# A graph network on one core: one fixed item per tile of nodes, edges counted by comparing keys, own rows added by VectorE

## The chip, the cores and the metric

The kernel runs on one core of one Trainium2 chip. The metric is the device time of one execution in microseconds, the median of several runs. The engines are TensorE (PE, its weight loads PEld), VectorE (DVE), ScalarE (ACT), GpSimd (POOL) and SyncE (SP), whose queue issues most transfers.

## The reference, cut

Four layers on 50,000 nodes with 256 features and 25,000 edges (src, dst, two edge types, a weight), each followed by a layer norm of input plus output. What the change touches is the second and the third.

```
def rgcn_layer(x, src, dst, edge_type, W, root, bias):      # twice
    xj = x[src]; out = x @ root + bias
    for r in range(16):
        mask = (edge_type == r)
        s = segment_sum(xj * mask[:, None], dst)
        cnt = segment_sum(mask, dst)
        h = s / maximum(cnt, 1.0)[:, None]
        out = out + blockdiagonal(h, W[r])
...
rel_e = relation_emb[edge_type]
def agg(x):                                                  # two hops
    e = sum((concat(x[head], x[tail]) @ fc_w.T + fc_b) * rel_e)
    e = where(e > 0, e, 0.2 * e)
    ex = exp(e - segment_max(e, head)[head])
    w = ex / segment_sum(ex, head)[head]
    return segment_sum(x[tail] * w[:, None], head) + x
for _ in range(2):
    x = agg(x); x = x / maximum(norm(x), 1e-12)
```

## The kernel before

**Items.** The nodes lie in 391 tiles of 128. `sort_edges` sorts the edges by src (`by_src`) and by dst (`by_dst`) into items: an item is up to 128 edges that all have their node in one tile. A tile with more than 128 edges would have several items, one behind the other, and an empty tile has one. With the given edges no tile has more than 128 of them, so there are 391 items for 391 tiles. `Tables.make` works out on VectorE, for each of 640 possible items and both graphs, its tile (LOAD), where its result is stored (STORE), the last item of its tile (LAST) and whether it goes on with the sum of the item before (`keep`); `Tables.number` adds SLOT, the tile's place in its octet of eight. Everything behind reads these tables into registers, since where a tile's items lie depends on the edges.

**Stages.** They run one after the other, each in a block of its own: the sort with weights, `mean_layer` (l0), `count_edges_and_message` (ma), `relation_layer` (l1a), `message_phase` (mb), `relation_layer` (l1b), `attention_hop` twice (l2a, l2b), `interaction_layer` (l3).

**ma.** 216 chunks of 128 edges in pairs: GpSimd gathers rows of x (L1098) into 24 landing slots, TensorE turns them (L1220) and multiplies by the blocks of the edge type (L1229), ScalarE copies between the two, VectorE copies the products out (L1120), and SyncE stores them. mb does the same for the second layer (L1329 to L1397) with filler matmuls `keep_busy` (L772) between. In ma the edges of each node and type are counted beside this. For the first 48 pairs a group of 8 items is made into one-hot matrices (L1111, L1106), multiplied (L1244) and copied to `total` (L1191); 8 pairs carry 16 scans over `total` (L1160), which add up the items of a tile; in 48 more pairs each edge looks its count up: a transposed one-hot (L1125) by the totals (L1253), masked by type (L1130) and reduced (L1133). At the end the share is 1 over the count (L1179).

**Hops.** `attention_hop` works on octets (8 items), two octets being one hop of the loop; 48 octets are written out, two more run in a loop with registers, and `steps` is the written order of each engine, with how many octets each step runs ahead. Per octet: `find_nodes` compares the row of node names (L2057, L2059); `look_up` gets each edge's head projection (L2320); `scores` adds the gathered one (L2070 to L2077); `spread` lays masked scores out by node (L2298, L2300); `maximum` takes the peak (L2126) and carries a running maximum over the items of a tile (L2130 to L2143); `chances` is exp with an accumulated sum (L2212); `turn_chances` turns it back (L2307); `aggregate` multiplies by the gathered rows (L2288). The node's own row is added in `add_self` (L2100) on VectorE in the first hop and in `own_rows` on TensorE in the second, by a diagonal that GpSimd makes (L2025); `guarded` (L2083) is its weight. `add_up` (L2121, in the second hop L2118) adds the sum of the item before, shrunk by the change of the maximum (0 where a new tile begins). `measure` (L2199) and `InverseRoot` (L2147, L1721 to L1738) give the norm. The second hop adds the residual (L2155) and a layer norm. GpSimd gathers eight items per octet (L1989), each half of them when TensorE has aggregated the octet that lay there two octets before.

## Time and profile before

| | us |
|---|---|
| median of 3 timed runs | 6657.72 (6646.8 to 6664.31) |
| profiled execution, span | 6924.1 |
| PE / PEld / DVE / ACT / POOL busy | 6036.3 / 5008.9 / 5018.1 / 4517.3 / 3702.0 |

The profiled execution has one time, its span, which is 4% above the median of the timed runs. Busy shares of the span (87% for PE) are averages over nine stages with different limits, and are read stage by stage.

### The profile page before, as it was taken

The numbers are of one execution on the slowest core, as the hardware profiler recorded it, in microseconds if no ns is written. First come the engines' busy times: TensorE is split into PE (matmuls) and PEld (weight loads), VectorE is DVE, ScalarE is ACT, GpSimd is POOL, SyncE is SP. The second block draws the span as 40 slices with busy tenths as digits, with TensorE's granted clock in tenths as the row PEclk, the third lists the DMA queues.
The fourth block names the chain that finished last, engine by engine and source line by source line (L and its number), as shares of the span: only waits on it lengthen the run. The fifth ranks groups of instructions, "written<-read, shape, count | busy, mean of one in ns | idle before, by whom it ended". The sixth has DMA issues, their size and how long they took to land. (4 is left out here: it accounts for less than half of the span.)

```text
span 6924.1 us, 154954 instructions
## 1 busy us (share of the span) xinstructions
PE 6036.3 (87%) x34664; PEld 5008.9 (72%) x34665; DVE 5018.1 (72%) x17037; ACT 4517.3 (65%) x15396; POOL 3702.0 (53%) x3473
## 2 busy tenths in 40 slices
PE   6437999977899987899999788887888887999999
PEld 2226999966877775699999666665776766888888
DVE  9786999976555551277777677775666666898898
ACT  1866999952144441178888566665777776777777
POOL 0766777756366666544444444444554455444444
PEclk9658999988899998999999899998989998999999
DMA  1025777765566665577777566665666665444444
GB/s 39 2 6 162 211 210 211 211 187 163 164 184 189 192 182 166 163 215 220 218 221 219 167 203 201 198 200 158 206 198 194 196 203 175 117 127 125 126 126 119
DMA packets 1158773, 1173.00 MB, mean 169 GB/s; under 512 B 301535, under 2 KB 1032838, under 8 KB 1157701
## 3 DMA queue, kind: packets, MB, share of 16 engines
q1 hardware_dynamic: 1007108, 953.00, 45.3%
q0 software_dynamic: 151360, 216.47, 12.4%
q8 instruction: 127, 2.08, 0.1%
q14 instruction: 178, 1.45, 0.1%
HBM read 961.43 MB, written 392.14 MB: 195 GB/s over the span
## 5 line engine op out<-in xcount | busy, mean ns | idle before, releaser
L214 POOL DMA_INDIRECT landing_first<-messages,by_dst_meta x768 | 842.7, 1097 | 721.8 <-PE l1b_ps_b L1541 366.5
L214 POOL DMA_INDIRECT landing_last<-x,by_dst_meta x384 | 434.4, 1131 | 561.0 <-PE l_ps_a L1678 487.9
L1989 POOL DMA_INDIRECT landing_last<-z,by_src_meta x408 | 424.3, 1040 | 521.3 <-PE l2b_ps_g L2288 366.6
L1989 POOL DMA_INDIRECT landing_last<-x,by_src_meta x408 | 422.7, 1036 | 462.4 <-PE l2a_ps_g L2288 255.9
L214 POOL DMA_INDIRECT landing_first<-in_x,by_src_meta x384 | 407.7, 1062 | 196.7 <-PE l_ps_a L993 74.4
L1495 ACT ACTIVATE l1a_x_t<-l1a_ps_x,by_dst_first 128x256 f32<-128x256 f32 x400 | 168.0, 471 | 418.0 <-PE l1a_ps_x L1527 280.0
L1539 PE MATMUL l1b_ps_b<-root,l1b_x_t 128*128 128x256 f32 x1600 | 426.9, 389 | 1.4
L1539 PE MATMUL l1a_ps_b<-root,l1a_x_t 128*128 128x256 f32 x1584 | 418.1, 386 | 9.7 <-issue 6.1
L1003 PE MATMUL l_ps_b<-l_w,l_both 128*128 128x256 f32 x1624 | 419.3, 381 | 0.0
L1006 PE MATMUL l_ps_b<-l_w,l_agg_t 128*128 128x256 f32 x1624 | 418.0, 380 | 0.0
L1697 PE MATMUL l_ps_b<-l_w,l_mix_t 128*128 128x256 f32 x1592 | 396.6, 392 | 10.2 <-issue 7.7
L1447 DVE SCALAR_TENSOR_TENSOR l1a_total<-l1a_total,by_dst_keep,l1a_ps_b 128x256 f32<-128x256 f32 x394 | 187.1, 475 | 292.1 <-PE l1a_ps_b L1541 234.5
L1693 PE MATMUL l_ps_b<-l_w,l_x_t 128*128 128x256 f32 x1592 | 382.2, 383 | 2.5 <-ACT l_x_t L1658 2.5
L1697 PEld LDWEIGHTS l_ps_b<-l_w,l_mix_t 128*128 128x128 f32 x1592 | 286.2, 189 | 115.7 <-DVE l_mix_t L1614 63.1
L288 POOL DMA_INDIRECT item_records<-sort_rec,places x196 | 218.5, 1115 | 243.8 <-DVE places L596 184.5
L1006 PEld LDWEIGHTS l_ps_b<-l_w,l_agg_t 128*128 128x128 f32 x1624 | 309.6, 191 | 42.5
L1098 POOL DMA_INDIRECT landing_first<-x,rel_index x216 | 238.7, 1105 | 164.4 <-PE ma_ps_x L1220 83.9
L1539 PEld LDWEIGHTS l1a_ps_b<-root,l1a_x_t 128*128 128x128 f32 x1584 | 286.3, 191 | 55.0 <-issue 18.9
L772 PE MATMUL l2a_ps_g<-zero_row,ones_b 128*128 128x392 bf16 x1734 | 321.2, 329 | 1.1 <-issue 1.1
L1003 PEld LDWEIGHTS l_ps_b<-l_w,l_both 128*128 128x128 f32 x1624 | 294.1, 191 | 32.1
L1539 PEld LDWEIGHTS l1b_ps_b<-root,l1b_x_t 128*128 128x128 f32 x1600 | 289.6, 191 | 36.5 <-issue 3.7
L1693 PEld LDWEIGHTS l_ps_b<-l_w,l_x_t 128*128 128x128 f32 x1592 | 286.6, 190 | 33.8 <-ACT l_x_t L1658 2.9
(399 smaller groups left out, 19392.5 us busy)
## 6 DMA issues: line engine op xcount, KB each, us to landing
l_both<-in_x_both SPq DMA_DIRECT2D x416, 256.0 KB
l2a_x<-x SPq DMA_DIRECT2D x53, 1216.0 KB
z<-l2a_result SPq DMA_DIRECT2D x400, 152.0 KB
x<-l1b_result SPq DMA_DIRECT2D x392, 152.0 KB
l2b_x<-z SPq DMA_DIRECT2D x53, 1024.0 KB
l1b_x<-h SPq DMA_DIRECT2D x408, 128.0 KB
l1b_res<-x SPq DMA_DIRECT2D x408, 128.0 KB
l2b_res<-x SPq DMA_DIRECT2D x51, 1024.0 KB
```

The costliest lines, as they stand in the source:

```text
L214: pool.indirect_dma_start(gathered[:, slot, 0:D], None, source[0:count, :], bass.IndirectOffsetOnAxis(ap=rows, axis=0), bounds_check=limit ...
L288: self.pool.indirect_dma_start(self.target, bass.IndirectOffsetOnAxis(ap=self.place[:, column:column + 1], axis=0), self.source(column), N ...
L772: pe.matmul(spare, c.ones_b[:], c.zero_row[:], start=True, stop=True)
L1003: pe.matmul(ps_b[k % 4], x_t[:, m, i * P:(i + 1) * P], w[:, 2 + i, :], start=(i == 0), stop=False)
L1006: last = pe.matmul(ps_b[k % 4], agg_t[:, k, i * P:(i + 1) * P], w[:, i, :], start=False, stop=(i == 1))
L1098: pool.indirect_dma_start(gathered[:, slot, :], None, x_in[0:N_NODES, :], bass.IndirectOffsetOnAxis(ap=relations.index[:, chunk:chunk + 1] ...
L1447: dve.scalar_tensor_tensor(total[:, k, :], total[:, (k - 1) % RING, :], graph.keep[:, bass.ds(j, 1)], ps_b[k // 2 % 2][:, k % 2, :], ALU.m ...
L1495: act.activation(x_t[:, k, :], ps_x[k // 2 % 2][:, k % 2, :], ACT.Copy, scale=graph.first[:, bass.ds(j, 1)]).then_inc(s["xt"], 1)
L1539: pe.matmul(sums, x_t[:, k, f * P:(f + 1) * P], root[:, f, :], start=(f == 0), stop=False)
L1693: pe.matmul(ps_b[k % 4], x_t[:, k, i * P:(i + 1) * P], w1[:, i, :], start=(i == 0), stop=False)
L1697: last = pe.matmul(ps_b[k % 4], mix_t[:, k, i * P:(i + 1) * P], w2[:, i, :], start=False, stop=(i == 1))
L1989: pool.indirect_dma_start(gathered[:, k, :], None, x_in[0:N_NODES, :], bass.IndirectOffsetOnAxis(ap=rows, axis=0), bounds_check=limit, oob ...
```

## The change

Every tile now has exactly one fixed item, whose number is the tile's. Only tiles with more than 128 edges get items behind them (from 392 on), so the first 48 octets know their tile when the code is written: loads of x, heads and residual use constants, and no running sum or maximum is carried there. The possible items rise from 640 to 896, and SLOT and `Tables.number` go. In ma 384 items are counted by comparing keys (node times 16 plus type) of an item's 128 edges with each edge's own, 4 compares behind each copy; the remaining group keeps the old way, in a loop ahead of the pairs, and fillers stand where look-ups stood. In the second hop the own rows move to VectorE, as in the first. Some buffers now share memory with others that are idle at that time (in l0 and the sort).

```diff
-MAX_ITEMS = TILES + N_EDGES // P
+MAIN = TILES + 1
+MAX_ITEMS = MAIN + 2 * (N_EDGES // (P + 1))
...
+OCTETS_FIXED = HOPS_FIXED * 2
...
# Tables.make
+            for q in range(whole, ITEM_CHUNKS):
+                chain.step(dve.tensor_scalar(self.junk[:, 0:n], b["end"][:, 0:n], c.item_id[:, q:q + 1], 0.0, ALU.is_le, ALU.add,
+                                             accum_out=self.tile_id[:, o, q:q + 1]))
...
             for q in range(ITEM_CHUNKS):
-                chain.step(dve.tensor_scalar(self.junk[:, 0:n], b["end"][:, 0:n], item, 0.0, ALU.is_le, ALU.add,
-                                             accum_out=self.tile_id[:, o, q:q + 1]))
                 for what, out in (("base", self.base), ("end", self.end)):
...
# count_edges_and_message, VectorE
+                def compare(g, odd):
+                    if not odd:
+                        dve.wait_ge(key_in[g % 2], (g // 2 + 1) * 16)
+                    for k in range(odd * HALF, (odd + 1) * HALF):
+                        j = g * RING + k
+                        if j >= 2:
+                            dve.wait_ge(s["compared"], j - 1)
+                        dve.tensor_scalar(same[:, j % 2, :], key_row[:, g % 2, k, :], key[:, j:j + 1], 0.0, ALU.is_equal, ALU.add,
+                                          accum_out=graph.share[:, j:j + 1]).then_inc(s["compared"], 1)
...
-                for pair in range(SCANNED, LOOKED):
-                    take_message(pair)
-                    g = pair - SCANNED
-                    look_and_take(g, g % 2, g // 2)
...
+                for pair in range(SCANS_AT, PAIRS_ALL):
+                    take_message(pair)
+                    g, odd = divmod(pair - FIRST_LOOK, 2)
+                    if 0 <= g < FAST_GROUPS:
+                        compare(g, odd)
# the same, TensorE
-                    if pair < COUNTED:
-                        count(pair)
-                    elif SCANNED <= pair < LOOKED:
-                        look_up(pair - SCANNED, (pair - SCANNED) % 2)
+                    if SCANS_AT <= pair < PAIRS_ALL - 8:
+                        keep_busy(pe, c, ps_spare, 3)
                     if pair + 2 < PAIRS_ALL:
                         turn(pair + 2)
+                    if SCANS_AT <= pair < PAIRS_ALL - 8:
+                        keep_busy(pe, c, ps_spare, 3)
...
# attention_hop, SyncE
+                def load_tiles(octet, target, source, columns, loads):
+                    if octet.general:
+                        rows = rows_of("load", LOAD, octet)
+                        for q in range(OCT):
+                            sp.dma_start(target[:, q, :], source[bass.ds(rows[q], P), columns]).then_inc(loads[1][octet.half], 16)
+                    else:
+                        tiles = source[bass.ds(octet.item * P, OCT * P), :].rearrange("(k p) d -> p k d", p=P)
+                        sp.dma_start(target, tiles[:, :, columns]).then_inc(loads[0][octet.half], 16)
...
# GpSimd
-                    pool.tensor_tensor(diag[:, 0:own_pe, :], c.ident[:].unsqueeze(1).broadcast_to([P, own_pe, P]),
-                                       guarded[:, octet.half, 0:own_pe].unsqueeze(2).broadcast_to([P, own_pe, P]), ALU.mult)\
-                        .then_inc(s["diag"], 1)
...
# VectorE
-                        dve.scalar_tensor_tensor(like_sums(q, z[:, k, :]),
-                                                 like_sums(q, x[:, bass.ds(at[q] + o.base, 1), :].rearrange("p k d -> p (k d)")),
+                        dve.scalar_tensor_tensor(like_sums(q, z[:, k, :]), like_sums(q, x[:, k, :]),
                                                  guarded[:, o.half, q:q + 1], sums(q), ALU.mult, ALU.add).then_inc(s["mixed"], 1)

                 def add_up(o, h):
+                    if not o.general:
+                        return
...
                 def maximum(o):
...
+                    if not o.general:
+                        o.wait(dve, s["peak"])
+                        dve.tensor_scalar(below[:, o.half, :], peak[:, o.both], -1.0, -FLOOR, ALU.mult, ALU.min)\
+                            .then_inc(s["below"], 1)
+                        return
...
# TensorE, second hop
-                    steps = [(find_slots, 3), (find_own, 1), (part(own_rows, 0), 1), (part(aggregate, 0), 1), (part(own_rows, 1), 1)]
...
+                    steps = [(part(aggregate, 0), 1), (part(aggregate, 1), 1), (part(aggregate, 2), 1), (spread, 2), (part(aggregate, 3), 1),
+                             (part(fill, 16), 2), (part(turn_chances, 0), 2), (look_up, 3), (part(fill, 4), 2),
+                             (part(turn_chances, 1), 2), (part(fill, 4), 2)]
```

VectorE in ma, in the part where edges look their counts up. Before, one pair and its group of 8 items:

```order
L1120 COPY ma_message<-ma_ps_m 128x512
L1125 TENSOR_SCALAR ma_hot_t<-ma_row,item_id 128x1024
L1106 TENSOR_TENSOR ma_kind<-by_dst_meta,iota 128x128
L1130 TENSOR_TENSOR ma_own<-ma_kind,ma_ps_e 128x128
L1133 TENSOR_REDUCE by_dst_share<-ma_own 128x8
L1120 COPY ma_message<-ma_ps_m 128x512
```

Now, two pairs, with the compares of one group of 8 items between them:

```order
L1153 COPY ma_message<-ma_ps_m 128x512 x2
L1163 TENSOR_SCALAR ma_same,by_dst_share<-ma_key_row,ma_key 128x128 x4
L1153 COPY ma_message<-ma_ps_m 128x512
L1163 TENSOR_SCALAR ma_same,by_dst_share<-ma_key_row,ma_key 128x128 x4
L1153 COPY ma_message<-ma_ps_m 128x512
```

Per pair 4 compares of 128 elements stand where a 1024-element compare, a type mask, a product and a reduction stood for 8 items; a group's compares now span two pairs.

VectorE in the first hop, from the third sum of an octet to the end of its maximum. Before:

```order
L2100 SCALAR_TENSOR_TENSOR l2a_z<-l2a_x,l2a_guarded,l2a_ps_g 128x304
L2121 SCALAR_TENSOR_TENSOR l2a_z<-l2a_z,l2a_shrink 128x304 x3
L2126 TENSOR_REDUCE l2a_peak<-l2a_ps_e 128x8
L2130 SCALAR_TENSOR_TENSOR l2a_top<-l2a_restart,l2a_top,l2a_peak 128x8
L2133 TENSOR_TENSOR l2a_old_top<-l2a_top,l2a_restart 128x8
L2135 TENSOR_SCALAR l2a_below<-l2a_top 128x8
L2137 TENSOR_SCALAR l2a_empty<-l2a_top 128x8
L2140 TENSOR_TENSOR l2a_minus<-l2a_old_top,l2a_top 128x8
L2143 COPY l2a_top<-l2a_top 128x1
```

Now, from the weight of the own row (`guarded`) on:

```order
L2101 SCALAR_TENSOR_TENSOR l2a_guarded<-l2a_peak,l2a_share 128x8
L2114 SCALAR_TENSOR_TENSOR l2a_z<-l2a_x,l2a_guarded,l2a_ps_g 128x304 x3
L2132 TENSOR_REDUCE l2a_peak<-l2a_ps_e 128x8
L2135 TENSOR_SCALAR l2a_below<-l2a_peak 128x8
L2114 SCALAR_TENSOR_TENSOR l2a_z<-l2a_x,l2a_guarded,l2a_ps_g 128x304 x4
L2114 SCALAR_TENSOR_TENSOR l2a_z<-l2a_x,l2a_guarded,l2a_ps_s 128x304
```

The running sums L2121 are gone, and only the peak and its negation are left of the maximum.

TensorE in the second hop, at the start of an octet. Before (TENSOR_LOAD and ISA rows are its sequencer reading slots and waiting):

```order
L1831 TENSOR_LOAD by_src_table x2
L1834 ISA
L2275 ISA
L2275 MATMUL l2b_ps_g<-l2b_x,l2b_diag 128x256
L2275 ISA
L2275 MATMUL l2b_ps_g<-l2b_x,l2b_diag 128x256
L2288 MATMUL l2b_ps_g<-landing_last,l2b_hot 128x256 x2
L1834 ISA
L2275 ISA
L2275 MATMUL l2b_ps_g<-l2b_x,l2b_diag 128x256
```

Now, the whole pass up to the first turn of chances:

```order
L2277 MATMUL l2b_ps_g<-landing_last,l2b_hot 128x256 x6
L2287 MATMUL l2b_ps_e<-l2b_mask,ident_b 128x512
L2289 MATMUL l2b_ps_e<-ident,l2b_score 128x128 x4
L2287 MATMUL l2b_ps_e<-l2b_mask,ident_b 128x512
L2289 MATMUL l2b_ps_e<-ident,l2b_score 128x128 x4
L2277 MATMUL l2b_ps_g<-landing_last,l2b_hot 128x256 x2
L788 MATMUL l2b_ps_spare<-zero_row,ones_b 128x392 x16
L2296 MATMUL l2b_ps_e<-ident,l2b_chance 128x128 x4
```

The products with `l2b_diag` and the register reads are gone; six aggregations stand in a row, then the spread, the last two and 16 fillers.

## Rows read from the trace of the kernel before

**Rows 1.** Windows by stage: length, busy us by engine, PEclk, DMA share, GB/s.

```profile
1467.00:1893.00 426.00, 324.19 (x2498) 300.57 (x2498) 253.10 (x531) 83.11 (x216) 238.68 (x216) 0.81 0.58 169
...
2600.00:2935.00 335.00, 264.97 (x1872) 209.68 (x1872) 73.69 (x108) 60.15 (x108) 214.28 (x212) 0.95 0.54 162
...
3828.00:4770.00 942.00, 803.37 (x5060) 609.93 (x5060) 688.08 (x1779) 604.18 (x2315) 444.74 (x430) 0.96 0.63 191
...
4770.00:5871.00 1101.00, 956.76 (x5186) 757.40 (x5186) 734.91 (x2420) 815.43 (x3207) 552.55 (x532) 0.90 0.64 194
```

**Rows 2.** Groups by line, counting stage: busy us, mean ns, idle before.

```profile
L1120 DVE COPY ma_message<-ma_ps_m 128x512 f32<-128x512 f32 x108 | 74.1, 686 | 84.2 <-PE ma_ps_m L1229 53.7 <-remote 20.5 <-issue 9.5
...
L1179 DVE RECIPROCAL by_dst_share<-by_dst_share 128x640 f32<-128x640 f32 x1 | 4.2, 4152 | 0.0
```

**Rows 3.** Timeline, ends of both message stages: start us, duration us.

```profile
1468.70 1.01 POOL L1098 DMA_INDIRECT landing_first<-x,rel_index  x1 [23.25 <-POOLq L123]
...
1896.63 0.27 DVE L1477 MEMSET l1a_total<- 128x256 f32 x1 [0.85 <-PEq L123]
...
2594.95 1.01 POOL L1329 DMA_INDIRECT landing_first<-h,rel_index  x1 [9.29 <-POOLq L123]
...
2931.25 0.69 DVE L1397 COPY mb_message<-mb_ps_m 128x512 f32<-128x512 f32 x1 [0.44 <-PE mb_ps_m L1350]
```

**Rows 4.** Groups by line, first hop, 3900 to 4700 (46 octets).

```profile
L2121 DVE SCALAR_TENSOR_TENSOR l2a_z<-l2a_z,l2a_shrink 128x304 f32<-128x304 f32 x365 | 195.8, 536 | 23.3
...
L2070 DVE TENSOR_TENSOR l2a_both<-l2a_ps_s,landing_last 128x192 f32<-128x192 f32 x46 | 16.4, 358 | 35.1 <-DMA landing_last<-x,by_src_meta 28.9 <-issue 5.8
...
L2147 DVE TENSOR_SCALAR l2a_inv_v<-l2a_total_sq 128x8 f32<-128x8 f32 x46 | 7.9, 172 | 40.9 <-ACT l2a_squares L2199 40.9
```

**Rows 5.** Timeline, two passes of the first hop, VectorE and GpSimd.

```profile
4215.83 0.36 DVE L2070 TENSOR_TENSOR l2a_both<-l2a_ps_s,landing_last 128x192 f32<-128x192 f32 x1 [0.35 <-DMA landing_last<-x,by_src_meta]
...
4222.74 1.01 POOL L1989 DMA_INDIRECT landing_last<-x,by_src_meta  x1 [1.41 <-PE l2a_ps_s L2288]
...
4226.69 1.28 POOL L1989 DMA_INDIRECT landing_last<-x,by_src_meta  x1 [0.31 <-issue]
...
4233.06 0.36 DVE L2070 TENSOR_TENSOR l2a_both<-l2a_ps_s,landing_last 128x192 f32<-128x192 f32 x1 [1.18 <-DMA landing_last<-x,by_src_meta]
```

**Rows 6.** Groups by line, second hop, 4850 to 5800 (46 octets).

```profile
L2275 PE MATMUL l2b_ps_g<-l2b_x,l2b_diag 128*128 x724 | 194.8, 405 | 19.2 <-POOL l2b_diag L2025 17.4 <-issue 1.6
...
L2025 POOL TENSOR_TENSOR l2b_diag<-ident,l2b_guarded 128x1024 f32<-128x1024 f32 x46 | 87.7, 1906 | 3.6
...
L2147 DVE TENSOR_SCALAR l2b_inv_v<-l2b_total_sq 128x8 f32<-128x8 f32 x46 | 47.7, 1037 | 88.4 <-ACT l2b_squares L2199 38.9 <-DMA x<-l1b_result 38.2 <-issue 11.3
```

**Rows 7.** Timeline, second hop, one VectorE step and the diagonal beside it.

```profile
5211.70 1.85 DVE L2147 TENSOR_SCALAR l2b_inv_v<-l2b_total_sq 128x8 f32<-128x8 f32 x1 [1.27 <-issue]
...
5211.63 1.90 POOL L2025 TENSOR_TENSOR l2b_diag<-ident,l2b_guarded 128x1024 f32<-128x1024 f32 x1
```

**Rows 8.** Table of two neighbouring octets of the second hop.

```profile
5181.60:5200.30 18.70, 16.99 (x102) 13.25 (x101) 12.37 (x45) 12.02 (x47) 10.66 (x11) 1.00 0.61 187
...
5200.30:5224.50 24.20, 21.03 (x101) 16.96 (x101) 16.56 (x51) 18.27 (x74) 10.35 (x11) 0.79 0.61 183
```

**Rows 9.** Timeline, TensorE in these two octets.

```profile
5189.28 1.86 PE L2320 MATMUL l2b_ps_s<-l2b_head,l2b_hot_t 128*128 x16
...
5208.75 0.66 PE L2307 MATMUL l2b_ps_e<-ident,l2b_chance 128*128 128x128 f32 x4 [2.56 <-ACT l2b_chance L2212]
...
5210.82 3.45 PE L2320 MATMUL l2b_ps_s<-l2b_head,l2b_hot_t 128*128 x16
```

**Rows 10.** Tables of the sort: one wide step (by line), one small (timeline).

```profile
L376 DVE TENSOR_SCALAR_CACHE_REDUCE sort_in_relation<-dst_end,item_id 128x391 f32<-128x391 f32 x5 | 3.1, 620 | 3.5 <-remote 2.2 <-DVE by_src_groups L396 1.3
...
371.33 0.17 DVE L386 TENSOR_SCALAR sort_vals<-sort_end 128x5 f32<-128x5 f32 x1 [1.23 <-DVE sort_vals L385]
```

**Rows 11.** Timeline, SyncE's queue in the first hop: eight issues of one store.

```profile
4703.77 4.88 SPq L1939 DMA_DIRECT2D z<-l2a_result  x8
```

More of the change, by code:

```diff
@@ L413, in turn @@
         sp.wait_ge(s_rows, 160)
[L415 to L423 removed]
+        sp.wait_ge(s_table, 32)
 def by_item(records):
@@ L1082, in _ @@
                             .then_inc(row_in[h], 16)
-                for h in range(2):
-                    sp.wait_ge(row_in[h], ((groups + 1) // 2 + 1) * 16)
-                    sp.sem_inc(s["passed"], 1)
+                for pair in range(SCANS_AT, PAIRS_ALL):
+                    store(pair)
+                    g, odd = divmod(pair - FIRST_LOOK, 2)
+                    if odd and 0 <= g < FAST_GROUPS - 2:
+                        load_keys(g + 2)
+                with sp.Fori(FAST_GROUPS // 2, (groups + 1) // 2) as both:
+                    for h in range(2):
+                        sp.wait_ge(row_in[h], (both + (2 - FAST_GROUPS // 2)) * 16)
+                        sp.sem_inc(s["passed"], 1)
                 for n in range(R // 2):
@@ L1742, with __init__ @@
 class Octet:
-    def __init__(self, group, n):
+    def __init__(self, group, n, general=None):
         self.number = group * 2 + n
@@ L1752, in __init__, with landed @@
         self.dynamic = not isinstance(self.number, int)
+        self.general = general if self.dynamic else self.number >= OCTETS_FIXED
+        assert self.general is not None
+    def landed(self, loads):
+        if self.general:
+            return loads[1][self.half], (self.lap + (1 - HOPS_FIXED)) * (16 * OCT)
+        return loads[0][self.half], (self.lap + 1) * 16
     def each(self):
@@ L1826, in attention_hop @@
         restart = ph.sb("restart", [P, ITEMS], F32)
-        diag = ph.sb("diag", [P, OCT, P], F32) if own_pe else None
         res = ph.sb("res", [P, OCT, D], F32) if last_hop else None
-        def load_slots(eng, regs, octet):
-            eng.load(regs, graph.table[0:1, SLOT, bass.ds(octet.item, OCT)])
-        def slots_of(eng, regs):
-            return [eng.snap(r, min_val=0, max_val=OCT - 1) for r in regs]
         ps_e = ph.ps("e", [P, OCT, P])
@@ L1924, in load_heads @@
                         sp.sem_inc(s["passed"], 1)
-                    sp.dma_start(head[:, octet.both, :], tiles[:, :, D + R2:]).then_inc(in_head[octet.half], 16)
+                    load_tiles(octet, head[:, octet.both, :], x_in, slice(D + R2, ROW), in_head)
                 def load_res(octet):
-                    tiles = tiles_of("res", octet, residual)
                     if octet.after(1):
@@ L1931, in load_res @@
                         sp.sem_inc(s["passed"], 1)
-                    sp.dma_start(res[:], tiles[:, :, 0:D]).then_inc(in_res[octet.half], 16)
+                    load_tiles(octet, res[:], residual, slice(0, D), in_res)
                 def store(octet):
@@ L2202, in decay @@
                 def decay(o):
+                    if not o.general:
+                        return
                     o.wait(act, s["minus"])
```

443 lines of the change are left out of this document (198 added, 245 removed).

## The prediction

> **What bounds the kernel now.** I read the table of stages first [rows 1]. The stages run one after the other, and the change touches the sort, the counting stage and both hops. In each row the reader is to see the busy time of every engine beside the length of the stage, then the granted TensorE clock. ScalarE, VectorE and GpSimd are full in none; TensorE is the fullest engine in both hops (803 of 942 us, 957 of 1101 us), but in the counting stage it is only 76% busy, at clock 0.81. So I went on stage by stage, to the groups by line and then to the order in time.
>
> The counting stage (1467 to 1893) and the second message stage (2600 to 2935) do the same 108 pairs of products from the same 216 gathers; only the first also counts edges. From the first gather to the end of the last copy the pure stage takes 2594.95 to 2931.94, 337.0 us or 3.12 a pair. The counting stage takes from 1468.70 to 1896.63, where the next stage's first instruction starts, 427.9 us [rows 3]. The difference is what counting costs.
>
> In the first hop one octet follows the other at 17.23 us (the same VectorE step at 4215.83 and 4233.06 [rows 5]); the window gives 942 us / 53 passes = 17.8 (50 octets and 3 lead-in passes). Two loops have this length. One is VectorE's own order, in which the running-sum step L2121 takes 8 x 536 ns = 4.3 us per octet [rows 4]. The other goes through GpSimd: gathers released at 4222.74, the fourth issued at 4226.69, VectorE waiting 1.18 us for its landing until 4233.06 [rows 5], then score, spread, aggregation and the next release. VectorE waits for landings 28.9 us in 46 octets [rows 4], so neither loop alone sets the pass.
>
> In the second hop a pass takes 1101 / 53 = 20.8 us. Per octet TensorE is busy 957 / 50 = 19.1 us, ScalarE 815 / 50 = 16.3, VectorE 14.7 [rows 1]. Two neighbouring octets show the two forms of a pass: 18.7 us at clock 1.00 and 24.2 us at 0.79 [rows 8]. In the long one the turn of the chances comes 2.56 us late, and then the same 16 look-up matmuls take 3.45 us in place of 1.86 [rows 9]. TensorE is the bound, and waiting for ScalarE makes it slower still. GpSimd's diagonal, 1906 ns, lies over a VectorE instruction on 8 elements that takes 1.85 us, where the first hop's takes 0.17 [rows 4, 6, 7].
>
> **The change part by part.** *Sorting and tables.* The wide VectorE steps at 128x391, about 0.62 us each [rows 10], go from 5 x 3 to 4 + 7 x 2 per graph, 30 to 36 in all: +4. The chain of small steps grows by about 28 in the tables and 8 in the buckets. One costs 0.17 us of work, and 1.4 with the wait for its neighbour's result [rows 10]: 36 x 0.17 = 6 to 36 x 1.4 = 50 us. About a third of these steps wait fully, so I take 14, and 2 for record loads that are 1.4 times as long: **+20** (10 to 50). GpSimd waits for the places that come out of the buckets and hides nothing of their part; of the tables it hides what is done before its last scatter. The removed numbering of octets runs beside those scatters and gives nothing back.
>
> *Counting stage.* 48 of 49 groups lose one-hot count, scan and look-up, and get 8 compares of 128x128 each with an accumulated sum, 4 behind each copy of the later pairs. No row shows this form. The nearest is L376, the same operation at 391 elements, 0.62 us, which bounds it from above; 0.17, the price of a handful of elements, does from below [rows 10]. By element count between them: 0.17 + 0.45 x 128 / 391 = 0.32 us. VectorE then does 0.69 [rows 2] + 4 x 0.32 = 2.0 us a pair, under the 3.12 at which the pure stage goes; the gathers and TensorE cover it. At 0.66 with spacing a pair takes 3.3 and costs 0.2 x 96 = 19 us. Ahead of the pairs stand four more transposes and one counted group; the gathers run on meanwhile into 24 landing slots, so of that delay I take 3 (0 to 14). Behind them the share of 896 items in place of 640: 4.15 x 1.4 = 5.8 [rows 2], with small steps 7.5, and the last compares 1. End: 1468.7 + 337.0 + 3 + 7.5 + 1 = 1817.2 against 1896.6: **-79** (-90 to -45).
>
> *First hop.* L2121 goes for 48 octets, and with it running maximum, its old value, the reset and ScalarE's decay: about 5 us of VectorE per octet. Only what the gather loop leaves of that is worth something. There the landing takes 4233.06 - 4226.69 = 6.4 us from the fourth gather's issue. The 1216 KB load of x stands in the same engines and will be issued earlier, since it waits for the sums of the octet before. With the landing as now a pass is 17.2 (gain 0.6, all of it from slower passes than the one shown); with landings no longer late, TensorE's busy time bounds at 803 / 50 = 16.1 (gain 1.7). I take 17.0, nearer to the loop that the rows show: 0.8 x 50 = 40. At the hop's end the general form loads tile by tile. Eight issues of a store take 4.88 us on that queue [rows 11], and eight each for x and heads now stand between them, in two octets: +10. **-30** (-80 to +10).
>
> *Second hop.* Own rows leave TensorE: 194.8 / 46 = 4.2 us per octet [rows 6]. In the octet at full clock it was busy 17.0 of 18.7 us [rows 8], so 12.8 remain. VectorE takes the own row into the instruction that added the running sum before, so its count there stays. GpSimd loses the diagonal, and L2147 goes from 1037 back to 172 ns [rows 4, 6]. What is late next is ScalarE: 16.3 us of work per octet, less 0.2 for the decay, plus waits in its ring: about 17.0. TensorE will then stand still 4 us per octet, in pieces that can be as long as the 2.56 us behind which its clock fell [rows 9]. One such fall cost 24.2 - 18.7 - 2.6 = 2.9 us of stream [rows 8, 9]; the slack hides a part, and I add 1.3. So 18.3 in place of 20.8: 2.5 x 50 = 125. The end costs more than in the first hop, since the residual is loaded by tiles too: +15. **-110** (-205, at ScalarE's 16.3, to -45).
>
> *Sum.* +20 - 79 - 30 - 110 = -199 on the profiled span of 6924.1 us. The timed runs have a median of 6657.7, 0.962 of it, so -191: **6465 us**.
>
> **The rivals.** *The first hop stays on its gather loop* (chance 0.15), since the load of x, issued earlier, collides with the gathers. For it: VectorE already waits for landings. Against it: 28.9 us in 46 octets are little beside 5 us per octet. No gain there: 6465 + 40 x 0.962 = 6505 us.
>
> *The second hop stays at 20.8* (0.17): a loop through landing, score and spread, or TensorE's uneven clock, takes the place of the own rows. For it: this hop moves 194 GB/s over 20.8 us, and its engines' share of 0.64 would be 0.76 at 17.5 [rows 1]. Against it: passes of 18.7 exist with the own rows in them. 6465 + 120 = 6585 us.
>
> *The compares are dear* (0.07). At 0.85 us each, the 0.62 and a wait for the compare two before, a pair takes 4.1 us, and the 79 us are gone: 6541 us.
>
> *TensorE's clock stays down in the second hop* (0.03); this one ends on the other side. The counting stage shows clock 0.81 at 76% busy, the second message stage 0.95 at 79% [rows 1]; the new hop would be busy 13 of 17 us, 76%. If the engine stays at the lower of its two levels (1.2 GHz), 12.8 us double to about 26, a pass is 26 in place of 20.8, +260 us, and the sum is -199 + 125 + 260 = +186 on the span: 6837 us. It decides from a pass of 22.3 on, where the other gains are used up. The Trainium skill says in "TensorE: Matmul & The Clock Gate", part 1, that the lower level is the default and activity releases the upper one; by that rule less work on this engine is a danger in itself. This case's octets agree in that the clock falls behind an idle stretch [rows 8, 9]; the octet ahead of that stretch is at the full one, fillers and all.
>
> **How the numbers follow.** My forecast, each term within its bounds, has 0.56; the rivals 0.15, 0.17, 0.07 and 0.03; 0.02 is for what I have not thought of. The best bounds together would be 10 - 90 - 80 - 205 = -365, or 6307 us; the first three rivals reach 6505 to 6585. With no more than two in ten outside I keep 6355 to 6580. About 0.3% (20 us) is what a measurement of this kernel can tell from no change; all cases but the last are faster by more. Faster 0.95, same 0.02, slower 0.03.
>
> **What would show it.** The counting stage at 349 us, its copies 3.1 us apart, the 128-element compare near 0.32 us. The first hop at 17.0 a pass, with VectorE idle 4 us more per octet and waiting for landings. The second hop at 18.3 a pass, L2147 at 0.17 us, TensorE idle 4 us with its clock under 0.95. The tables 15 us longer. I am wrong if the compare takes over 0.6 us, if a pass of the second hop stays above 20, or if the hops' ends cost more than 40 us together.

## The result and the profile after

The changed kernel takes 6409.31 us (median of 4 runs, 6404.78 to 6418.08) against 6653.1 of the kernel before: ratio 0.9632, 95% interval 0.9619 to 0.9646, 244 us faster. The forecast was 6465. The page of its profiled execution begins so (span, then busy us by engine, with shares of the span):

```profile
span 6403.0 us, 147348 instructions
PE 5706.8 (89%) x33252; PEld 4755.8 (74%) x33253; DVE 4656.3 (73%) x16722; ACT 4458.0 (70%) x15208; POOL 3534.5 (55%) x3365
```

One thing has to be known for all that follows: the profile from which the forecast was made (span 6924.1) was of a disturbed execution, and a second profile of the same kernel has a span of 6639.6 us. So the stages are compared with that second profile. Its windows of the counting stage, the first hop and the second hop (each from the end of the stage ahead, or its own start, to the start of the next; length, busy us of PE, PEld, DVE, ACT, POOL, then PEclk, DMA share, GB/s), where [rows 1] had 426, 942 and 1101:

```profile
1415.70:1817.50 401.80, 316.37 (x2498) 297.31 (x2498) 253.65 (x531) 84.29 (x217) 243.53 (x216) 0.84 0.61 181
3669.80:4588.10 918.30, 772.76 (x5008) 601.30 (x5060) 685.93 (x1780) 609.16 (x2316) 440.56 (x430) 0.98 0.65 196
4588.10:5590.90 1002.80, 902.98 (x5134) 717.33 (x5186) 734.30 (x2421) 817.74 (x3207) 556.52 (x532) 0.94 0.70 213
```

The same three windows of the changed kernel:

```profile
1415.90:1723.90 308.00, 261.43 (x1902) 221.31 (x1902) 212.21 (x917) 67.57 (x125) 220.56 (x216) 0.92 0.80 238
3571.70:4444.60 872.90, 786.95 (x5060) 607.22 (x5060) 454.19 (x1179) 587.10 (x2268) 431.50 (x430) 0.97 0.68 206
4444.60:5355.50 910.90, 748.88 (x4370) 600.89 (x4370) 637.63 (x2280) 806.36 (x3159) 442.00 (x428) 0.89 0.78 234
```

The reader is to see 401.8 become 308.0, 918.3 become 872.9, and 1002.8 become 910.9. All other stages together, from the sort to the last layer, give 5.5 us. The sum is 6639.6 - 6403.0 = 237 us on the spans.

The sort shows why its term is missing. The second profile of before, the last VectorE step of the sort and GpSimd's last scatter:

```profile
456.53 0.48 DVE L422 TENSOR_SCALAR by_dst_table<-sort_rows_on 1x640 int32<-1x640 int32 x1
...
501.01 0.97 POOL L288 DMA_INDIRECT item_records<-sort_rec,places  x1 [0.30 <-issue]
```

And the changed kernel:

```profile
465.01 0.36 DVE L652 TENSOR_SCALAR rel_index<-sort_ps_source 128x216 int32<-128x216 f32 x1
...
500.11 0.96 POOL L289 DMA_INDIRECT item_records<-sort_rec,places  x1 [0.30 <-issue]
```

VectorE's last step starts 8 us later and has 35 us to spare before the scatters end; the next step waits for those, and they end within 1 us of where they did.

The counting stage in order of time (GpSimd's gathers, VectorE's copy of a pair, its first compares, the next gather and copy):

```profile
1600.21 1.00 POOL L1131 DMA_INDIRECT landing_first<-x,rel_index  x1 [0.30 <-issue]
...
1600.23 0.69 DVE L1153 COPY ma_message<-ma_ps_m 128x512 f32<-128x512 f32 x1 [0.57 <-PE ma_ps_m L1265]
...
1600.84 0.34 DVE L1163 TENSOR_SCALAR_CACHE_REDUCE ma_same<-ma_key_row,ma_key 128x128 bf16<-128x128 f16 x1
...
1601.10 0.34 DVE L1163 TENSOR_SCALAR_CACHE_REDUCE ma_same<-ma_key_row,ma_key 128x128 bf16<-128x128 f16 x1
...
1601.52 1.00 POOL L1131 DMA_INDIRECT landing_first<-x,rel_index  x1 [0.30 <-issue]
...
1602.56 0.69 DVE L1153 COPY ma_message<-ma_ps_m 128x512 f32<-128x512 f32 x1 [0.57 <-PE ma_ps_m L1265]
```

Gathers start 1.31 us apart, 2.6 a pair. Copies come 2.33 apart here, and 2.44 on average between 1500.4 and 1710.6 (86 steps), since the pairs, which started late, catch up with gathers that have already landed. While they catch up TensorE sets the pace, fillers and all: it is busy 100 us of the 100 from 1500 to 1600, and each copy waits 0.57 us for it. A compare starts 0.26 us behind the one before. Four of them and the copy fill 1.7 us, so VectorE is late in neither phase.

In the stage of before the pairs fall behind their gathers in the half in which edges look their counts up: the copy of pair 48 starts 8 us after the pair's second gather, that of pair 96 59 us after. The engine that is nearly full there is TensorE, with the look-ups (second profile, same columns as above):

```profile
1600.00:1750.00 150.00, 140.01 (x984) 136.85 (x985) 73.67 (x174) 20.15 (x35) 93.82 (x89) 0.81 0.69 195
```

TensorE is busy 140 of 150 us at a granted clock of 0.81, VectorE 74.

One pass of the second hop: the first residual sum, the score, TensorE's spread, the start of the layer norm's root (`inv_v`), the peak and its negation, the last exponential, ScalarE's guess of the root, and the first residual sum of the next octet:

```profile
4904.43 0.48 DVE L2165 SCALAR_TENSOR_TENSOR l2b_result<-l2b_z,l2b_inv_root,l2b_res 128x256 f32<-128x256 f32 x1 [0.27 <-DVE l2b_inv_root L1780]
...
4909.21 0.17 DVE L2091 SCALAR_TENSOR_TENSOR l2b_score<-l2b_plain 128x8 f32<-128x8 f32 x1
...
4909.43 0.39 PE L2287 MATMUL l2b_ps_e<-l2b_mask,ident_b 128*128 128x512 bf16 x1 [1.80 <-DVE l2b_score L2091]
...
4913.01 0.17 DVE L2174 TENSOR_SCALAR l2b_inv_v<-l2b_norm_squares 128x8 f32<-128x8 f32 x1 [1.58 <-ACT l2b_norm_junk L843]
4913.09 1.22 DVE L2132 TENSOR_REDUCE l2b_peak<-l2b_ps_e 128x8 f32<-128x1024 f32 x1
...
4914.34 0.17 DVE L2135 TENSOR_SCALAR l2b_below<-l2b_peak 128x8 f32<-128x8 f32 x1
...
4917.31 0.39 ACT L2226 ACTIVATE l2b_chance<-l2b_ps_e,l2b_below 128x128 f32<-128x128 f32 x1
...
4919.85 0.30 ACT L1765 ACTIVATE l2b_inv_y<-l2b_inv_log,shift 128x8 f32<-128x8 f32 x1
...
4921.02 0.48 DVE L2165 SCALAR_TENSOR_TENSOR l2b_result<-l2b_z,l2b_inv_root,l2b_res 128x256 f32<-128x256 f32 x1 [0.27 <-DVE l2b_inv_root L1780]
```

This is a ring over three engines, 4904.43 to 4921.02, 16.59 us, in which each row comes after the one above it, by a result that it needs or by its place in the order of its engine (L2174 alone does not need the spread). Ahead of the peak two branches meet, and the later one counts: TensorE's spread, which ended at 4911.81 in this pass, and ScalarE's eight squares for the layer norm (L843), for which L2174 waits 1.58 us here. From 4524.6 to 5224.6 (42 passes) VectorE waits 49.0 us for those squares, and behind that still 22.4 us for the spread, in 26 of the passes.

The engines in these 700 us (same columns):

```profile
4524.60:5224.60 700.00, 597.69 (x3523) 480.21 (x3524) 509.41 (x1836) 662.29 (x2599) 348.45 (x335) 0.91 0.82 248
```

ScalarE is busy 95% of them, TensorE 85%, VectorE 73%. Over the whole hop ScalarE has only 806 of 911 us, because the passes at its start and end are not full. So there are two limits of nearly one length: ScalarE's own work, and the ring.

### The profile page after: what moved, and what is told of

Its sections match the earlier page's. It is cut to its first block and busy times, and to the rows that moved or that the text cites. A ratio compares the mean times of both kernels' runs of the same rounds, so it can differ in the third digit from the quotient of the medians.

```text
span 6403.0 us, 147348 instructions
## 1 busy us (share of the span) xinstructions
PE 5706.8 (89%) x33252; PEld 4755.8 (74%) x33253; DVE 4656.3 (73%) x16722; ACT 4458.0 (70%) x15208; POOL 3534.5 (55%) x3365
## 3 DMA queue, kind: packets, MB, share of 16 engines
q14 instruction: 169, 1.38, 0.1%
## 5 line engine op out<-in xcount | busy, mean ns | idle before, releaser
L215 POOL DMA_INDIRECT landing_first<-messages,by_dst_meta x768 | 828.3, 1079 | 657.2 <-PE l1b_ps_b L1583 367.2
L2027 POOL DMA_INDIRECT landing_last<-x,by_src_meta x408 | 409.3, 1003 | 404.8 <-PE l2a_ps_g L2277 245.2
L843 ACT ACTIVATE l_norm_junk<-l_summed,l_norm_minus_mean 128x256 f32<-128x256 f32 x392 | 196.0, 500 | 137.5 <-DVE l_norm_minus_mean L834 137.5
```

Source lines behind the costliest of these rows:

```text
L215: pool.indirect_dma_start(gathered[:, slot, 0:D], None, source[0:count, :], bass.IndirectOffsetOnAxis(ap=rows, axis=0), bounds_check=limit ...
L843: act.activation(self.junk[:, k % self.junk_slots, :], values[:, k, :], ACT.Square, bias=self.minus_mean[:, k:k + 1], accum_out=self.squar ...
L2027: pool.indirect_dma_start(gathered[:, k, :], None, x_in[0:N_NODES, :], bass.IndirectOffsetOnAxis(ap=rows, axis=0), bounds_check=limit, oob ...
```

## The experiments

All but the first are timed in rounds beside the kernel before; a ratio is to that kernel, with its 95% interval. The changed kernel itself has 0.9632 (0.9619 to 0.9646). The kernel before had medians from 6639.3 to 6653.1 us in these rounds, and by the intervals a difference between two ratios is known to some 15 us.

**The kernel before, again.** No edit.

> The kernel before, unchanged, profiled a second time. In the first profile the second message stage, which the change does not touch, took 337 us from first gather to last copy, and in the profile of the changed kernel 278. Theory A: that first profiled execution was a slow one as a whole, and its rows overstate stages that wait for gathers; then this span is near 6650 us, the second message stage near 280 and the counting stage near 370, so that the change gave the counting stage about 80 us. Theory B: the changed kernel makes untouched stages faster; then the second message stage stays near 337 here.

Span 6639.6, and 280 us for the second message stage (first to last TensorE instruction) where the first profile has 328. Theory A. The first profile overstated the stages that live on gathers, the hops included. The counting stage, expected near 370 us, has 402, so the change gave it 94 us and not 80.

**Room for 640 items.** The edit also gives back the two buffers of the first layer that shared memory:

```diff
-MAX_ITEMS = MAIN + 2 * (N_EDGES // (P + 1))
+MAX_ITEMS = MAIN + N_EDGES // (P + 1)
```

> The changed kernel with room for 640 items in place of 896 (enough for the given edges), and with it the two buffers of the first layer that had to share memory standing alone again. It tells what the wider tables cost. Theory of the prediction: two chunks fewer take 12 wide VectorE steps of 0.62 us off the tables, some 8 us, and 2 to 3 us off each load of records and off the closing share in the counting stage: 10 to 18 us faster than the changed kernel, about 6395 us. Rival: all of it is hidden beside GpSimd's scatters, under 4 us.

Ratio 0.9637 (0.9621 to 0.9653): no difference. The counting stage is 6 us shorter (302.2 in place of 308.0). In the sort VectorE is done 10 us earlier (455.1 in place of 465.4), and the stage behind starts only 2 us earlier (504.7 in place of 507.0). The rival holds for the tables.

**Own rows on TensorE, with the diagonal; the diagonal alone.**

```diff
+                    steps = [(part(own_rows, 0), 1), (part(aggregate, 0), 1), (part(own_rows, 1), 1),
+                             (part(own_rows, 2), 1), (part(aggregate, 1), 1), (part(aggregate, 2), 1), (part(own_rows, 3), 1),
...
                     gather_fixed(Octet(0, n))
+                    if own_pe and n > 0:
+                        diagonals(Octet(0, n - 1))
```

In both runs VectorE also gets back one compare of 8 elements per octet (`empty`, 0.17 us), which the diagonal's weight needs.

> As items640, but the second hop's own rows go back to TensorE, with GpSimd's diagonal and its weight as before; VectorE's sum keeps its instruction with a factor of 0, so that it does as many steps. Theory of the prediction: TensorE needs 4.2 us more per octet and the diagonal holds VectorE's step L2147 by 0.9 us; a pass grows by 2 to 2.5 us, 100 to 125 us over 50 octets, about 6500 us. Rival: ScalarE or the landings set the pass, and TensorE has room; then less than 30 us.

> As items640, but in the second hop GpSimd makes the weight and the diagonal of every octet again, and nothing reads them; the own rows stay on VectorE. Putting own rows back on TensorE with the diagonal cost 81 us against items640. This tells the two apart. Theory: the diagonal holds VectorE's small steps by 0.9 us and more in each octet, and it delays GpSimd's next gathers by 2.1 us; VectorE and ScalarE are now the longest, so half of the 81 us come back, 35 to 50. Rival: TensorE's 4.2 us alone made the 81, and the diagonal costs under 10.

Ratios 0.9756 (0.974 to 0.9772) and 0.9767 (0.975 to 0.9785): 79 and 86 us slower than items640, where 100 to 125 were expected of the first, and half of its loss of the second. The windows of the second hop, first items640:

```profile
4438.00:5346.50 908.50, 730.30 (x4318) 598.74 (x4370) 637.58 (x2279) 806.00 (x3159) 442.59 (x428) 0.90 0.78 234
```

own_rows_on_pe:

```profile
4443.80:5430.10 986.30, 855.68 (x5134) 704.64 (x5186) 690.39 (x2276) 809.65 (x3159) 542.61 (x532) 0.97 0.72 216
```

diag_only:

```profile
4446.10:5442.10 996.00, 762.19 (x4318) 635.65 (x4370) 722.96 (x2328) 814.36 (x3159) 555.30 (x532) 0.85 0.72 214
```

TensorE has 93 us more busy time in own_rows_on_pe than in diag_only, and the stage is 10 us shorter. So the matmuls of the own rows cost nothing on balance, and the diagonal (with its `empty`) all of it. They are not free work, though: they also do what fillers do. The spread's matmuls in the two windows, diag_only first:

```profile
L2313 PE MATMUL l2b_ps_e<-ident,l2b_score 128*128 128x128 f32 x832 | 182.1, 393 | 201.2 <-DVE l2b_score L2112 201.0
```

```profile
L2332 PE MATMUL l2b_ps_e<-ident,l2b_score 128*128 128x128 f32 x832 | 111.4, 278 | 10.2 <-DVE l2b_score L2117 7.5
```

The own rows (209 us busy) fill the wait for the scores, the granted clock is 0.97 in place of 0.85, and the spread behind them takes 278 ns in place of 393. No run tells their price from what they give back by the clock.

The timeline of the diagonal (diag_only: GpSimd's diagonal, and VectorE's first residual sum beside it):

```profile
4915.09 1.90 POOL L2065 TENSOR_TENSOR l2b_diag<-ident,l2b_weight 128x1024 f32<-128x1024 f32 x1
...
4915.20 2.07 DVE L2189 SCALAR_TENSOR_TENSOR l2b_result<-l2b_z,l2b_inv_root,l2b_res 128x256 f32<-128x256 f32 x1 [0.27 <-DVE l2b_inv_root L1779]
```

The first of the eight residual sums takes 2.07 us in place of 0.48, and ends with the diagonal. In other octets the diagonal falls on a step of the root with 8 elements (L1774), and holds that one as long. The two groups over the whole window:

```profile
L2189 DVE SCALAR_TENSOR_TENSOR l2b_result<-l2b_z,l2b_inv_root,l2b_res 128x256 f32<-128x256 f32 x400 | 212.5, 593 | 13.7 <-DVE l2b_inv_root L1779 13.3 <-DMA l2b_res<-x 0.4
...
L1774 DVE SCALAR_TENSOR_TENSOR l2b_inv_b<-l2b_inv_a,l2b_inv_v 128x8 f32<-128x8 f32 x101 | 48.0, 476 | 3.5
```

items640 has 167.3 and 16.8 us for them. VectorE's busy time grows by 722.96 - 637.58 = 85 us, of which 45 are residual sums, 31 this step of the root and 8 `empty`; the stage grows by 87.5. The held steps stand in the ring, and so does the spread, which takes 30 us more than in items640 (182.1 in place of 152.3) at the lower clock. Together that is more than the stage grew, so a part found slack; the runs do not divide it.

The held steps read two operands in SBUF. The Trainium skill ("GPSIMD Engine Reference", section 1, "Specifications") names contention between GpSimd and VectorE instructions with two SBUF inputs, and this trace agrees: in one octet the diagonal (4473.66 to 4475.56) lies over two products of VectorE, the first with one operand in PSUM, the second with both in SBUF:

```profile
4474.47 0.36 DVE L2105 TENSOR_TENSOR l2b_both<-l2b_ps_s,landing_last 128x192 f32<-128x192 f32 x1 [3.01 <-PE l2b_ps_s L2332]
...
4474.86 0.91 DVE L2108 TENSOR_TENSOR l2b_own<-l2b_both,l2b_kind 128x192 f32<-128x192 f32 x1
```

Elsewhere both take 0.36 us.

**The whole old counting stage.** As items640, with `count_edges_and_message` of before, `total` for 640 items, and one clamp of the tables to match.

> As items640, but with the whole counting stage of the kernel before (one-hot counts, scans over 640 items, look-ups, no fillers). Theory of the prediction: the counting stage takes 80 us longer (75 to 95), about 6475 us. Rival: the gathers were the limit of both and the change gave at most 45 us there.

Ratio 0.9777 (0.9761 to 0.9794), 93 us slower than items640. The window (items640: 302.2 us, clock 0.93):

```profile
1412.60:1807.90 395.30, 307.59 (x2498) 288.50 (x2498) 253.22 (x532) 84.67 (x217) 238.14 (x216) 0.85 0.62 184
```

395.3 against 302.2, at clock 0.85. The theory, at the upper end of its range (75 to 95).

**Every compare twice.**

```diff
-                        if j >= 2:
-                            dve.wait_ge(s["compared"], j - 1)
+                        for again in range(2):
+                            if 2 * j + again >= 2:
+                                dve.wait_ge(s["compared"], 2 * j + again - 1)
...
```

> The changed kernel, with each of the 384 compares of the counting stage done twice (the second sum goes to a buffer that nobody reads). One compare measured 0.27 us from start to start. A pair takes 2.60 us, two gathers at 1.31 us. Theory: VectorE's 0.69 + 4 x 0.27 = 1.8 us are hidden behind the gathers; twice, 0.69 + 8 x 0.27 = 2.85 us are not, so the stage grows by 0.25 us in each of 96 pairs, 24 us (10 to 30), and not by the 104 us of work added. Rival: the compares are on the path already; then 90 to 104 us.

Ratio 0.9686 (0.967 to 0.9703), 36 us slower than the changed kernel. The window:

```profile
1416.00:1751.30 335.30, 277.94 (x1902) 213.56 (x1902) 305.95 (x1684) 67.51 (x124) 219.98 (x216) 0.93 0.71 219
```

VectorE works 94 us more (305.95 against 212.21), and the stage takes 27.3 us more, as expected (24, 10 to 30). The single compare is off the path, and the point from which it would bound lies between one and two.

**Running sums back in the first hop.**

```diff
-                    if not o.general:
+                    if not (carry or o.general):
                         return
```

> As items640, but the first hop carries sums and maxima in all octets again (its loads keep their constants). In the second profile of the kernel before, the first hop took 918 us from the end of the stage ahead to the start of the second hop, and in the changed kernel 873. Theory of the prediction: the running sums were one of two loops of about the same length; putting them back costs 40 us or a little more (30 to 55), about 6445 us. Rival: the gather loop holds and the 45 us came from the constant loads on SyncE's queue; then under 10 us.

Ratio 0.9696 (0.9678 to 0.9713), 39 us slower than items640. The window:

```profile
3563.60:4487.10 923.50, 776.83 (x5008) 608.51 (x5060) 681.08 (x1779) 603.88 (x2316) 441.23 (x430) 0.97 0.65 195
```

923.5 against 875.5, and 918.3 in the kernel before: the whole difference of that stage comes back with the sums, and the constant loads give nothing. The 39 us lie in the expected range (30 to 55).

What VectorE waits for in that stage (total, times, longest), the kernel before (second profile) and then the changed one:

```profile
DVE l2a_both L2070 <- DMA landing_last<-x,by_src_meta: 50.7, 50, 6.6
```

```profile
DVE l2a_inv_v L2158 <- ACT l2a_squares L2211: 237.3, 51, 5.2
...
DVE l2a_both L2084 <- DMA landing_last<-x,by_src_meta: 31.3, 41, 7.6
```

The waits for landings did not grow when the sums went, they fell. VectorE now stands for ScalarE's squares, 237.3 us, for which it waited 30.0 before.

**Fewer fillers in the first hop.**

```diff
-(part(aggregate, 3), 1), (part(fill_late, 20), 1), (part(turn_chances, 0), 2),
+(part(aggregate, 3), 1), (part(fill_late, 12), 1), (part(turn_chances, 0), 2),
```

> The changed kernel, with 12 filler matmuls in place of 20 behind the aggregation in the first hop. There ScalarE waits 69 us in 48 octets for TensorE's turn of the chances, so the fillers may stand in the way. Theory: TensorE with its fillers is the bound of the first hop now (15.7 of 16.2 us busy); 1.3 us less gives 0.5 to 1.0 a pass, 25 to 50 us. Rival: the gather loop is the bound, and fewer fillers give nothing, or let the clock fall and cost time.

Ratio 0.9687 (0.9668 to 0.9705), 37 us slower than the changed kernel. The window, and the spread's matmuls (the changed kernel has 872.9, clock 0.97, and 278 ns for the same group):

```profile
3568.70:4484.10 915.40, 747.46 (x4600) 602.82 (x4652) 454.57 (x1180) 586.61 (x2268) 430.32 (x430) 0.92 0.65 196
```

```profile
L2289 PE MATMUL l2a_ps_e<-ident,l2a_score 128*128 128x128 f32 x736 | 130.6, 337 | 117.8 <-DVE l2a_score L2091 117.8
```

TensorE waits 117.8 us for scores now (44.7 in the changed kernel), and behind that wait its spread runs at 337 ns. The theory expected 25 to 50 us of gain; what came is the rival, its second half: the fillers are not in the way, they keep the clock.

**The last layer-norm step split.** ScalarE keeps four rows of eight:

```diff
+                def apply_rest(o):
+                    pass_wait(dve, s, norm.shifted, o.number + 1)
+                    for j, k in o.each()[4:OCT]:
+                        dve.tensor_scalar(result[:, k, :], result[:, k, :], inv2.root[:, k:k + 1], norm.bias[:, k:k + 1],
+                                          ALU.mult, ALU.add).then_inc(s["out_ready2"], 1)
...
-(weigh, 1), (shift_bias, 0), (improve, 1)]
+(weigh, 1), (shift_bias, 0), (improve, 1), (apply_rest, 0)]
```

> The changed kernel, with the last step of the second hop's layer norm (scale and shift of 256 elements) split: ScalarE does four of the eight rows of an octet, VectorE the other four at the end of its order. ScalarE has 16.1 us of work in a pass of 17.0. Theory: ScalarE is now the bound of the second hop; it loses 2.4 us, VectorE gains 4 x 0.25 us, and a pass falls by 0.8 to 1.5, 40 to 75 us, about 6355. Rival: TensorE, whose granted clock is 0.89 there, or the landings are the bound as well; under 15 us.

Ratio 0.9699 (0.9682 to 0.9717), 44 us slower, where 40 to 75 us of gain were expected. ScalarE lost 90 us of work, and the stage grew from 910.9 to 960.0. The timeline on VectorE (the root, the new step, the first residual sum):

```profile
4903.98 0.17 DVE L1780 SCALAR_TENSOR_TENSOR l2b_inv_root<-l2b_inv_b,l2b_inv_y 128x8 f32<-128x8 f32 x1
...
4904.18 1.38 DVE L2190 TENSOR_SCALAR l2b_result<-l2b_result,l2b_inv_root,l2b_norm_bias 128x256 f32<-128x256 f32 x4
...
4905.47 0.48 DVE L2170 SCALAR_TENSOR_TENSOR l2b_result<-l2b_z,l2b_inv_root,l2b_res 128x256 f32<-128x256 f32 x1
```

The 1.38 us stand between the root and the residual sum, two rows that follow each other in the ring above. A pass grows from 16.59 to 17.7. This does not show that ScalarE was no limit: it is busy 95% of the middle of the hop before the split and 79% after (4520 to 5220), and now waits 97.7 us in 770 for the row means that come out of the residual sums. The split relieved one of the two limits and lengthened the other.

**Scores before the residual sums; the same with the split.**

```diff
-                    steps = [(add_residual, 0), (centre, 0), (scores, 2), (guard, 1),
+                    steps = [(scores, 2), (add_residual, 0), (centre, 0), (guard, 1),
```

> The changed kernel, with one step of VectorE's order in the second hop moved: the scores of the octet two ahead stand before the residual sums, not behind them. Theory, formed after the split of the last layer-norm step cost 37 us and the unread diagonal 86: the pass is one loop across the engines, in which VectorE's Newton steps, the residual sums (3.4 us), the scores, TensorE's spread, the peak, ScalarE's exponentials, four squares and its guess follow each other; all that stands in it counts in full. Then the residual sums leave the loop, and ScalarE's 16.1 us bound the pass of 16.6: 0.3 to 0.6 us a pass, 15 to 30 us, about 6385. Rival: ScalarE or the gathers hold the pass, nothing changes, or the spread cannot come earlier because the aggregations before it wait.

> scores_first together with the split of the last layer-norm step (four of eight rows on VectorE), which alone made the changed kernel 37 us slower. By the theory of one loop the VectorE steps that were added now stand outside of it, and ScalarE has 13.8 us of work per pass, VectorE 15.3: a pass of 15.5 to 16, 40 to 60 us faster than the changed kernel, about 6360. Rival: VectorE's added 1.4 us stand in the loop here too; then it is slower than scores_first by 20 us or more.

Ratios 0.9853 (0.9836 to 0.9869) and 0.9838 (0.9821 to 0.9854), 147 and 137 us slower than the changed kernel, where a gain was expected of both; neither the theories nor their rivals had this. VectorE's wait for landings over 700 us of the second hop (total, times, longest), scores_first:

```profile
DVE l2b_both L2084 <- DMA landing_last<-z,by_src_meta: 80.5, 26, 5.1
```

The changed kernel:

```profile
DVE l2b_both L2084 <- DMA landing_last<-z,by_src_meta: 3.0, 8, 0.7
```

The residual sums gave the gathers the time to land. With the scores in front of them VectorE stands still for the landing, 2.2 us on average over the 36 octets of the window, and all that is queued behind it comes late, the residual sums too. ScalarE's squares for the layer norm, which need those sums, come late in turn: VectorE waits 89.8 us for them, in the changed kernel 49.0. The ring through the gathers, a rival in the prediction, lies close behind the ring that bounds. The split gives 10 us there, inside the two intervals.

**Fillers before the spread in the second hop.**

```diff
-(part(aggregate, 2), 1), (spread, 2), (part(aggregate, 3), 1),
+(part(aggregate, 2), 1), (part(fill, 10), 2), (spread, 2), (part(aggregate, 3), 1),
```

> The changed kernel, with 10 filler matmuls (1.65 us) in the second hop where TensorE waits for the scores, 2.5 us per octet, before the spread. In the changed kernel the granted clock is 0.89 there, and the spread's matmuls take 346 ns in place of 275. Theory: that stretch of TensorE lies in the loop; with fillers the clock stays up, the spread takes 0.5 to 1 us less, and a pass falls by as much, 25 to 50 us, about 6370. Rival: the fillers are late as often as early, and the gain is under 10 us or a loss.

Ratio 0.9612 (0.9595 to 0.9628); that of the changed kernel is 0.9632, and the two intervals overlap. The window of the stage, the middle of the hop, and the spread's matmuls:

```profile
4442.00:5332.10 890.10, 790.81 (x4890) 602.71 (x4890) 635.24 (x2279) 801.37 (x3159) 439.17 (x428) 0.95 0.80 239
```

```profile
4522.00:5222.00 700.00, 644.79 (x4048) 490.40 (x4049) 523.77 (x1897) 678.22 (x2674) 357.20 (x346) 0.98 0.84 255
```

```profile
L2289 PE MATMUL l2b_ps_e<-ident,l2b_score 128*128 128x128 f32 x693 | 93.2, 278 | 0.0
```

The same group of the changed kernel:

```profile
L2289 PE MATMUL l2b_ps_e<-ident,l2b_score 128*128 128x128 f32 x672 | 123.8, 346 | 0.0
```

The stage falls from 910.9 to 890.1 us, by 21, where 25 to 50 were expected. The clock rises from 0.89 to 0.95, and the spread's 16 matmuls, each 68 ns shorter, lie in the ring: in the 700 us VectorE's wait for them ahead of the peak falls from 22.4 us to 0.8. What holds the pass then is, by its busy time, ScalarE (678 of 700 us, 97%); no run was made on that. By its profile and by its ratio it is the fastest kernel of the study, but its lead of 13 us in the timed runs is less than the intervals can tell.

## Why the prediction was right, and where it was not

The forecast was 6465 us (6355 to 6580), and 6409 came. On the spans it said 199 us of gain, and 237 came. Two of its errors took each other out, and that is luck: the sorting cost 20 us less than forecast, and the second hop gave 18 less. None of the four rivals came: the compare takes 0.34 us, both hops are shorter, and the clock of the second hop is 0.89.

- **Sorting and tables, +20: measured about 0.** The work did grow, by 8 us up to VectorE's last step. The step that failed is "about a third of these steps wait fully, so I take 14": the tables hide behind GpSimd's scatters, which the text said of a part only. In the second profile 45 us lie between the last table step and the end of the scatters. (By its own prices a third would also be 12 x 1.4 + 24 x 0.17 = 21, not 14.)
- **Counting stage, -79: measured -94**, and -93 with only this part undone. The sum was of the right form: the pure stage plus what is left of the counting. The compare came at 0.34 us of length and 0.27 from start to start, forecast 0.32, and stayed hidden. The term that was mis-sized is the pair: 337.0 us for 108, 3.12 each, from a disturbed profile. The same rows in the second profile of before:

```profile
2495.32 1.01 POOL L1329 DMA_INDIRECT landing_first<-h,rel_index  x1 [9.55 <-POOLq L123]
...
2783.05 0.69 DVE L1397 COPY mb_message<-mb_ps_m 128x512 f32<-128x512 f32 x1 [0.43 <-PE mb_ps_m L1350]
```

  That is 288.4 us, 2.67 a pair. With the prediction's own 11.5 us for the rest the sum gives 299.9 us from the first gather to the next stage, against 395.4 in that profile: -95. The first profile had stretched the pure stage by 49 us and the counting stage by only 33.
- **First hop, -30: measured -45**, 48 with the sums put back on the profile and 39 in time. The choice that failed is "I take 17.0, nearer to the loop that the rows show", the loop through the landings: VectorE's waits for landings fell from 50.7 to 31.3 us, and what came up were 237 us of waits for ScalarE's squares. The pass went from 17.3 us (918.3 / 53) to 16.5 (872.9 / 53), near the other bound of the text, TensorE's 16.1. What bounds it now is not shown: fewer fillers made it longer. The hop's end with loads by tile was put at 10 us; the runs do not show it apart.
- **Second hop, -110: measured -92.** The size is near, the main cause is not, so this too is luck. "Own rows leave TensorE: 4.2 us per octet" was the main term, and those matmuls were worth nothing on balance. "TensorE is the bound" was the false step behind it. The diagonal was priced at 0.9 us on a step of 8 elements, again from the disturbed profile; in the second one it falls on a residual sum instead (mean 619 ns, 482 in the changed kernel). In diag_only it held steps in the ring by about 1.5 us an octet, and it was worth 78 to 88 of the 92 us. "What is late next is ScalarE" was right in the main: it is busy 95% of the middle of the hop, and its 16.3 us of work per octet lie just under the pass that came, 16.6. It is not the only limit, as the split shows. "18.3 in place of 20.8" started from passes of the disturbed profile.
- **TensorE's clock.** The 1.3 us added for it were of the right kind (granted clock 0.89, forecast under 0.95) and too large. What fillers ahead of the spread give back is 20.8 us of the stage, 0.4 us a pass, because the spread is the later branch in 26 of 42 passes.
- **The factor 0.962** took the disturbance as evenly spread. The spans of the undisturbed profiles differ by 237 us, the times by 244.

What stays open: why the first profile was slow; what bounds the first hop now; how the 78 to 88 us divide between held steps and clock; and how much of the second hop's last 4 to 14 us is the running maximum. No run takes that apart.

## What to carry to other kernels

Before a step is priced by the busy time of its engine, follow one pass from row to row until it closes, and look at every place where two branches meet for the one that ends last. Take the busy shares from the middle of the stage: over the whole hop ScalarE looked 89% busy, in the middle it was at 95%. Work that is moved off a nearly full engine is a loss if it lands in the ring (the split, 49 us of the stage), and work on TensorE that fills a wait can give back by the clock what it costs (the own rows). Price a helper on GpSimd by what it holds on VectorE, not by its own length. Profile the kernel before twice when its span and the timed median differ by some per cent.

## What the runs showed of the hardware

- A GpSimd product over 128x1024 elements (1.90 us) stretched VectorE instructions with two SBUF operands: from 0.48 to 2.07 us (diag_only, 4915.20), from 0.36 to 0.91 (4474.86). The product just before that one, with an operand in PSUM, lay wholly beside the diagonal and stayed at 0.36.
- 128 elements of float16 compared and summed take 0.34 us, and the next one starts 0.26 us after it.
- Eight filler matmuls less per octet (of 34) brought the granted clock of the first hop from 0.97 to 0.92 and cost 42 us; ten more in the second hop brought it from 0.89 to 0.95 and gave 21.
